# Earlier row statistics, a later wait for the spread keys, and another spacing of the running maxima in a perceiver layer

## The reference, cut to what matters

```python
x = x + xattn(ctx_1024, layernorm(x), mask)   # 16 heads of 64, queries from x, keys and values from ctx and x
x = x + attn(layernorm(x))                    # 16 heads of 8 over the 64 rows, with a linear bias ("alibi")
x = x + ffn(layernorm(x))                     # int8-like fake quantisation, silu gate

def xattn(x, latents, mask, ...):
    xn, ln = layernorm(x, g_x, b_x), layernorm(latents, g_l, b_l)
    q, kv = ln @ Wq, concat(xn, ln) @ Wkv
    sim  = where(mask, q k^T * scale, -max)
    attn = softmax(sim)                       # needs a bound of each query's scores: the "maxima"
    return layernorm((attn @ v) @ Wout, g_o, b_o)
```

## Time and profile before

| | |
|---|---|
| median of 3 runs | 810.05 us (809.28 to 811.12) |
| the profiled execution | 812.56 us, its span 810.8 us |
| busy in the span | PE 93%, ACT 75%, DVE 69%, POOL 67% |
| mean granted TensorE clock | 0.978 of full speed |
| chain that ended last | PE 65%, DVE 14%, issue 10%, ACT 5%, POOL 3% |
| loop | bodies 2 to 14, from 124.8 us to 700.7 us |

### The profile page before, as it was taken

The page is one execution under the profiler, slowest core; times in us unless marked ns, Lnnn a source line. Parts: engine busy times, 40 slices in busy tenths (PEclk is TensorE's granted clock), DMA queues, the critical chain, the costliest instruction groups (busy, mean ns, idle before and its releaser), DMA issues.

```text
span 810.8 us, 22755 instructions
## 1 busy us (share of the span) xinstructions
PE 751.5 (93%) x7122; PEld 418.6 (52%) x7122; DVE 559.9 (69%) x1399; ACT 609.7 (75%) x1086; POOL 545.3 (67%) x745
## 2 busy tenths in 40 slices
PE   5598999999999999999999999999999999899766
PEld 3344544556464555545554655555555546455423
DVE  5776776666666767666666667676766666586677
ACT  5479788887868687888878696868788887865262
POOL 4366676686867768686868677686868686766122
PEclk9799999999999999999999999999999999999797
DMA  5303322121222202121212212121212121110001
GB/s 178 79 6 93 78 75 73 43 61 56 57 60 56 58 17 63 45 71 42 63 52 58 58 55 62 32 58 32 71 45 72 40 60 56 47 43 19 4 1 53
DMA packets 95820, 44.42 MB, mean 55 GB/s; under 512 B 66500, under 2 KB 87848, under 8 KB 95656
## 3 DMA queue, kind: packets, MB, share of 16 engines
q1 hardware_dynamic: 95728, 43.93, 19.5%
q10 hardware_dynamic: 56, 0.05, 0.0%
HBM read 24.20 MB, written 3.34 MB: 34 GB/s over the span
## 4 chain that ended last, share of the span: by engine, by line
PE 65%; DVE 14%; issue 10%; ACT 5%; POOL 3%; DMA 1%; DVEq 1%; ACTq 0%; SPq 0%; POOLq 0%
PE bank L1496 14%; PE bank L1576 7%; PE bank L1459 6%; PE bank L1463 5%; PE bank L1461 5%; PE bank L1414 4%; PE bank L1593 3%; DVE mx L1940 3%; PE bank L1431 3%; PE bank L1611 2%; PE bank L1390 2%; DVE qkl_l L1936 2%; PE bank L1430 2%; PE bank L1648 1%; ACT qkl_h L1118 1%
## 5 line engine op out<-in xcount | busy, mean ns | idle before, releaser
L867 POOL TENSOR_TENSOR p<-arena,p 128x512 f16<-128x512 f32 x256 | 297.9, 1169 | 133.0 <-ACT arena L1137 131.9
L1146 ACT ACTIVATE p<-bank,maskbias 128x512 f16<-128x512 f32 x224 | 155.2, 693 | 103.5 <-PE bank L1463 101.5
L1496 PE MATMUL bank<-p,xv 128*128 128x512 f16 (+1 forms) x768 | 182.3, 380 | 5.3 <-POOL arena L915 3.7
L1940 DVE TENSOR_REDUCE mx<-bank 128x1 f32<-128x464 f32 x256 | 154.0, 632 | 17.8 <-PE bank L1431 16.1
L1137 ACT ACTIVATE arena<-bank,maskbias 128x512 f32<-128x512 f32 x224 | 155.0, 692 | 0.0
L1496 PEld LDWEIGHTS bank<-p,xv 128*128 128x128 f16 (+1 forms) x768 | 58.2, 97 | 74.5 <-issue 25.6
L1936 DVE TENSOR_TENSOR qkl_l<-bank,qkl_h 128x512 f16<-128x512 f32 x64 | 41.1, 686 | 68.9 <-ACT qkl_h L1118 68.8
L1459 PE MATMUL bank<-qkc_h,xtT_h 128*128 128x512 f16 (+1 forms) x256 | 86.5, 389 | 0.0
L1463 PE MATMUL bank<-qkc_h,xtT_l 128*128 128x512 f16 (+1 forms) x256 | 85.0, 379 | 0.0
L1461 PE MATMUL bank<-qkc_l,xtT_h 128*128 128x512 f16 (+1 forms) x256 | 85.0, 379 | 0.0
L1431 PE MATMUL bank<-xtT_h,qkc_h 128*128 128x400 f16 x256 | 83.4, 338 | 0.0
(11 more groups left out here) (283 smaller groups left out, 1576.0 us busy)
## 6 DMA issues: line engine op xcount, KB each, us to landing
arena<-den_dram SPq DMA_DIRECT2D x62, 128.0 KB, 3.2
qkc_h<-arena SPq DMA_DIRECT2D x30, 256.0 KB, 2.4
qkc_l<-arena SPq DMA_DIRECT2D x30, 256.0 KB, 2.5
raw<-in_ctx SPq DMA_DIRECT2D x32, 192.0 KB, 2.4
lt<-lt_dram SPq DMA_DIRECT2D x60, 32.0 KB, 2.1
arena<-in_L_xattn_Wkv SPq DMA_DIRECT2D x1, 1024.0 KB, 7.8
raw<-in_ctx SPq DMA_DIRECT2D x64, 8.0 KB, 2.0
ltT_dram<-x_all SPq DMA_DIRECT2D x4, 256.0 KB, 2.8
```

Of the source, the lines that this page charges most:

```text
L867: g.tensor_tensor(p_halves[0:r, slot, 1, :], p_all[0:r, (plan.halves_made(0, k, t) - 1) % 2, :], p_halves[0:r, slot, 0, :], ALU.subtract). ...
L1146: a.activation(p_halves[0:r, slot, 0, :], sbank[t % SRING][0:r, :], ACT.Exp, bias=bias)
L1496: op = mm(bk[:, :], halves_of[at, row, :], p_halves[at, slot, prob, :], start=tile < 2 and n == 0, stop=last and n == 2)
L1940: v.tensor_reduce(mx[:, hq_tile, part:part + 1], bk[:, 0:width], AX.X, ALU.max).then_inc(s_jobs_taken, 1)
```

## The change

Three edits, all but the first list of batches for the plan `WINDOW` alone. The statistics (`STATS` and `AGGR`) of the even batches move from step 4 to step 1 of the body, those of the odd batches from step 12 to step 8; for the first two batches they stay in step 4. The maxima of the even batches (`EVEN`) that were due at 10.5, 11, 11, 11.5, 12, 12, 12.5, 13 become due at 10.5, 11, 11.5, 12, 12, 12.5, 12.5, 13. On PE, `before_self_scores` moves from before `values` to behind `values` and the jobs of the quarter step.

```diff
-    STATS={4: (0, 4)}, AGGR=4, RSTD=5, XHAT=6, MASK=5,
+    STATS=[{1: (0, 4)}, {0: (0, 4)}, {4: (0, 4)}], AGGR=[1, 0, 4], RSTD=5, XHAT=6, MASK=5,
@@
-    EVEN=dict(T=[7.5], MAX=[10.5, 11, 11, 11.5, 12, 12, 12.5, 13], MT=14.25), XV={2: (0, 4)},
+    EVEN=dict(T=[7.5], MAX=[10.5, 11, 11.5, 12, 12, 12.5, 12.5, 13], MT=14.25), XV={2: (0, 4)},
@@ body of PE
                         prep(plan, i, last, s)
-                        background(plan, i, since, s, before_self_scores)
+                        if plan is WHOLE:
+                            background(plan, i, since, s, before_self_scores)
                         if t >= LAG:
                             values(plan, i, k, t - LAG)
                         elif since or k == 1:
                             values(plan, i - 1 + k, 1 - k, t - LAG + plan.STEPS)
                         prep(plan, i, last, s + 0.25)
+                        if plan is WINDOW:
+                            background(plan, i, since, s, before_self_scores)
                         prep(plan, i, last, s + 0.5)
@@ DVE
             def ahead(plan, n, par, t):
 
                 at, CH = plan.at, plan.CH
-                if t in at["STATS"]:
-                    if t == min(at["STATS"]):
+                which = 2 if isinstance(n, int) and n < 2 else par
+                if t in at["STATS"][which]:
+                    if t == min(at["STATS"][which]):
                         dve.wait_ge(s_ctx_loaded[par], ctx_count(plan, n, par))
                         if happened(n):
                             dve.wait_ge(s_ctx_rstd, n)
-                    for c in range(*at["STATS"][t]):
+                    for c in range(*at["STATS"][which][t]):
                         v.bn_stats(st[:, c, :], raw[:, par, c, :])
-                if t == at["AGGR"]:
+                if t == at["AGGR"][which]:
```

More of the change, by code:

```diff
@@ L171 @@
 WHOLE = Plan(0, ({0}, {0}), dict(
-    STATS={14: (0, 5), 15: (5, 9), 16: (9, 13)}, AGGR=17, RSTD=18, XHAT=20, MASK=21,
+    STATS=[{14: (0, 5), 15: (5, 9), 16: (9, 13)}] * 3, AGGR=[17] * 3, RSTD=18, XHAT=20, MASK=21,
     START=dict(QP=[-3, -3], QC=[-2, -2], QL=[-1, -1], T=[0.5, 1.5, 2.5, 3.5], MAX=[11 + m // 3 + 0.5 * (m % 3 > 0) for m in range(32)], MT=23),
```

## The result

The changed kernel takes **833.81 us** in the median of 4 runs (832.15 to 835.25) against 810.38 us (809.28 to 811.12) for the kernel before (4 runs): a ratio of 1.029, interval 1.0267 to 1.0313. It is 23.4 us slower; 19.0 were forecast.

What follows compares the result with a forecast made beforehand. PE was taken as the bound, busy 43.5 of 44.30 us per body. 13 x (0.48 + 0.58) = 13.8 plus 5.2 for the first bodies gave 19.0 us on 810.05: 829.0 us, range 824 to 834.

Steps and rivals of the forecast that it cites:

- the main forecast: Both mechanisms, late context rows and held `xh`, slow the kernel to 829.0 us, range 824 to 834; chance 0.58.
- the fifth rival: Waits are longer, rows landing 2.4 us after issue because DMAs bunch, +0.40 per body more: 834 to 836 us; chance 0.05.
- The moved wait: Step 1, PE: `values` starts at once, but QC still waits for DVE; counted 0, at most 0.24 us gain per body.
- Even statistics: Step 4 to 1: DVE waits for the third load, QC's taking 0.60 us late, PE's third maximum held; net +0.48 us per body.
- Odd statistics: Step 12 to 8: QL's taking 0.29 us late but PE not held; counted 0, upper bound +0.25 us.
- Maxima: Even batches: `xh` held by POOL's L867, fourth maximum behind it, PE's seventh late; net +0.58 us per body.
- the signs: List of what the profile after would show, including a PE wait of about 0.9 us ahead of the even batch's sixth maximum.
- The gain of 0.17 that the rivals granted: Maxima of even batches if `xh` is not held and takes 0.35 us: 0.17 us gain per body, used by rivals.
- Bodies 0 and 1: Step 8: late statistics and L1773 delay QL's taking; +2.8 us in body 0, +2.4 in body 1, together +5.2.
- the first four: Rivals: load in time, 804.7 (0.11); `xh` not held, 818.8 (0.11); only maxima cost, 821.8 (0.10); nothing reaches PE, 810 (0.05).

Runs made afterwards that it cites:

- the old maxima: Changed kernel with only the spacing of the even batches' maxima put back (10.5, 11, 11, 11.5, 12, 12, 12.5, 13): 825.80 us, ratio 1.0182.
- The earlier load: Changed kernel with SP's three loads of the context rows issued ahead of the spreading of the denominators (L680) in step 0: 825.77 us, ratio 1.018.
- both other causes undone: Changed kernel with the context rows loaded earlier in step 0 and the old spacing of the even maxima: 816.84 us, ratio 1.0079.
- three surroundings: New spacing of even maxima in the kernel before (830.64 us), in the changed kernel, and in a faster kernel with `xh` in step 13 (806.44 against 805.43 us).

## Why the prediction was right, and where it was too small

The measured 833.81 us lies 0.2 us inside the upper end of the range that the main forecast gave itself (824 to 834), and by the number alone the fifth rival (834 to 836) fits as well; only the runs tell which mechanism it was. That the number came to lie inside is in part luck, since one term was 4 us too small.

**The moved wait, 0.** Right. Alone it gains 1 us, 0.08 per body, near the 0.1 that was left of the 0.24 behind a semaphore's delay. In the changed kernel it is hidden by what follows it, as said.

**Even statistics, +0.48 per body.** Right in mechanism and nearly in size: the wait for the DMA, L1936 0.59 us late, the third maximum held. By the ruler they cost 0.58 us against the kernel before: 0.38 in the interval with step 1, and 0.20 in the other (32.59 against 32.39 with the old maxima), since what DVE does for the store that ends the first (L1965) is 0.37 us late where PE is 0.64 late. Two readings in the working were off. PE's first maximum was taken to be on time and is 0.35 us late. And two starts of maxima with nothing between them lie 0.25 us apart in 31 cases of the trace before and 0.20 in two, not 0.21: what is won back at the sixth maximum is some 0.09 us and not 0.13. The earlier load takes 8.0 us back, 0.62 per body. One thing behind the term I had not named: PE now hangs on a transfer in every body and takes over its scatter. Before, the interval with step 1 was 11.9 us in all but two of twelve bodies (12.0 and 13.0); after, eleven lie between 12.1 and 12.5 us and one at 13.8; with the earlier load they are back at 11.8 to 12.0. The body of 13.8 us is read on SP and DVE:

```profile
223.40 0.38 SPq L673 DMA_DIRECT2D den_dram<-rcol  x1
...
227.10 1.35 SPq L680 DMA_DIRECT2D arena<-den_dram  x2
...
231.96 0.88 DVE L1896 BATCH_NORM_STATS2 st<-raw 128x6 f32<-128x128 f32 x4 [2.81 <-DMA raw<-in_ctx]
```

L680 reads back what L673 stored, and was issued 3.7 us behind it, where the body of the first timelines has 2.2. What was late is the store: it landed 3.68 us behind its issue, where 25 of the 28 stores from 120 to 740 us took 1.41 to 1.46, and L680 was issued 0.02 us later. The loads behind it on SP are late with it, and DVE waits 2.81 us instead of 1.34. It explains little of the difference, though: the trace of before has its own such body, 13.0 us long, in which the same store landed after 2.96 us and PE waits 1.1 us for the transfer issued just ahead of it (`qkc_h` out of `mT`, L655).

**Odd statistics, 0.** Right. DVE waits 1.93 us for the DMA in step 8 and takes QL at once behind the statistics, 0.24 us later than before against the taking of T (forecast: 0.29), and PE is not late: with both other causes undone the loop runs at the speed of the moved wait alone.

**Maxima, +0.58 per body.** Right in mechanism and size (0.55 by the ruler). The working names PE's seventh maximum and the signs the sixth; the wait is at both, 0.69 us and 0.18. One part of it was loose: "while POOL is in L867, `xh` stands" holds for the one instruction that is running, not for a row of them. For the kernel before that makes no difference. The gain of 0.17 that the rivals granted to the spacing without the hold, for which the prediction shows no working, is not there.

**Bodies 0 and 1, +5.2 us.** This is the term that was mis-sized: 9.2 in place of 5.2 us, and I had called it an estimate that could be 2 us too high. For body 0 it had L1773 at 1.10 us behind the statistics and QL's taking 2.8 us late. I moved the instruction and kept its duration. In its new place its four instructions run beside four of POOL's in a row, L867, L896, L901 and L906, which keep POOL busy for 3.1 us (66.37 to 69.44), and take 3.43 us: the very hold that the prediction used for `xh`, in a shape of the same kind. Singly they last 1.27, 0.76, 1.31 and 0.33 us, and the first three end 0.08 us behind L867, L901 and L906. QL's taking starts at 69.70 instead of 63.99, 5.7 us late, 0.8 of it from ahead of step 8; PE, which had 0.7 us idle there, stands 5.6. That makes some 4.9 us of the 6.9. The rest comes behind it, in the stretch with the clock at 0.50: the same matmuls lie 5.70 us behind the trace before at 71.03 and 8.22 us behind it at 77.17, 2.5 us more, and PE's 5.17 us of work there would be about 2.6 at full clock, an estimate. Some 0.6 us of slack is taken back after that. Both go together when the old order of these bodies is restored (6.2 us less). How much of the 6.2 is the clock's alone was not measured apart. Body 1 was right (2.3 against 2.4).

**The sum.** The loop gave 14.2 where 13.8 were forecast, the first bodies 4.0 more than forecast, 0.8 came ahead of them, and the end gave back 1.4. Of the rivals, the first four are ruled out by the runs: the rows weren't there, `xh` was held, and the load alone is worth 8.0 us. The fifth is ruled out as well: the third load of the even batches lands 1.94 to 2.33 us behind its issue in the bodies of the loop, and 2.19 in the one of 13.8 us, where it was the issue that came late.

## What to carry to other kernels

An instruction that is moved doesn't keep its duration: look up what each engine that shares something with it is doing at the new place, for every instruction behind the insertion and not only for the one under discussion. Idle time of an engine is no free room for work whose data land in it: ask when the last byte is there, and put the issue forward first. A spacing of jobs is good or bad only together with what stands between them: the same edit cost 20.6, 8.0 and about 1 us in three surroundings.

## What the runs showed of the hardware

- **A VectorE `tensor_scalar` on f32 in SBUF ends 0.08 us behind the GpSimd instruction that it meets**, even if GpSimd has the next one ready: 0.35 us free, 1.17 beside one of 1.16 us, 1.17 again beside two in a row, 0.68 beside two of 0.65. One exception: in body 0 the second of the L1776 met the short L896 (0.19 us) and ended only behind L901, the one after it.
- **The hold works the other way too.** In step 6 four `tensor_scalar` of the rows (L1909) stand in a row on DVE. In the body of the first timelines L867 starts 0.27 us behind the start of the second; the second and third take 0.33 us each, and L867 takes 1.34 us instead of 1.16. The fourth starts 0.24 us behind L867 and takes 1.18.
- **`bn_stats` and the maxima are not stretched** in the same places: 0.27 to 0.30 us for a `bn_stats` that meets a GpSimd instruction, 0.26 to 0.29 for one that doesn't; 0.59 to 0.64 and 0.61 to 0.64 for a maximum.
- **One wait of 5.6 us on PE was followed by 5.2 us at 1.2 GHz** (granted clock 0.50 from 71.0 to 76.2 us, 0.89 in the stretch of the wait). Waits of under 1 us in every body left it at 1.00.
- **A small store to DRAM (L673) landed 1.41 to 1.46 us behind its issue in 25 of 28 cases, and after 3.68 us in one body**, with nothing in the kernel that differs there; in the trace before one took 2.96. The read that depends on it was issued 0.02 us behind the late landing each time.
